# One maximum product with each score, and the pieces beside the attention at other steps

## The reference, cut to what matters

```
x = x + tanh(g_xattn) * xattn(layernorm(x), ctx, ctx)      # 16 heads of 16
x = x + tanh(g_ffn)   * ffn(layernorm(x))
# xattn: q, k, v = projections; softmax(q k^T / 4) v, per head
# ffn:   q, k by weights and rope; softmax(q k^T / 4) v; Wo; rmsnorm;
#        shared SwiGLU + the two best of 8 experts; rmsnorm
```

## Time and profile before

| what | value |
|---|---|
| median of 3 runs | 774.14 us (774.02 to 775.43) |
| the profiled execution | 774.76 us |
| its span, first to last instruction | 772.7 us |
| PE busy | 738.2 us (96%) |
| DVE, ACT, POOL busy | 515.0, 408.4, 218.6 us |
| matmul instructions | 3490 |
| score and maximum products | 512 each |
| granted TensorE clock, mean over the span | 0.991 |

### The profile page before, as it was taken

How to read it: one execution, slowest core, us unless ns; L and a number is a source line. 1 busy time by engine, 2 the same in 40 slices (tenths; PEclk the granted TensorE clock), 3 DMA queues, 4 the chain that set the end, 5 groups by cost and what they waited for, 6 DMA issues and landing times.

```text
span 772.7 us, 10296 instructions
## 1 busy us (share of the span) xinstructions
PE 738.2 (96%) x3490; PEld 334.7 (43%) x3490; DVE 515.0 (67%) x774; ACT 408.4 (53%) x768; POOL 218.6 (28%) x327
## 2 busy tenths in 40 slices
PE   8869999999999999999999999999999999999995
PEld 5522343243233233233423332333544756468884
DVE  5769848956978878887797789771566222533765
ACT  4447868777767776875775867666211122222000
POOL 5332233214305414313321420010104631400444
PEclk9979999999999999999999999999999999999998
DMA  8782234316214513512331232005102565000011
GB/s 262 226 228 80 60 107 127 83 32 202 69 42 150 151 42 112 159 45 78 110 99 44 97 110 68 17 2 166 53 0 97 186 192 179 9 1 0 30 40 42
DMA packets 51891, 73.31 MB, mean 95 GB/s; under 512 B 7808, under 2 KB 42880, under 8 KB 51840
## 3 DMA queue, kind: packets, MB, share of 16 engines
q1 hardware_dynamic: 47248, 63.80, 28.3%
q0 software_dynamic: 2816, 8.46, 2.9%
q10 hardware_dynamic: 1776, 0.40, 0.3%
HBM read 45.04 MB, written 27.33 MB: 94 GB/s over the span
## 4 chain that ended last, share of the span: by engine, by line
PE 75%; DVE 13%; ACT 5%; issue 3%; DMA 2%; POOL 0%; SPq 0%; POOLq 0%; DVEq 0%; ACTq 0%
PE ps L1514 35%; PE ps L1667 12%; PE ps L1697 12%; PE ps L1639 10%; DVE negm L1161 7%; ACT hS L912 3%; PE ps L1509 2%; DVE bst L1039 2%; PE ps L1573 1%; PE ps L1653 1%; DMA w<-mTs 1%; DMA rows<-in_L_xattn_wq_dram 1%; PE ps L1568 1%; DMA w<-scrq 1%; DVE rows L1046 0%
## 5 line engine op out<-in xcount | busy, mean ns | idle before, releaser
L1161 DVE TENSOR_REDUCE negm<-ps 128x2 f32<-128x1024 f32 x256 | 303.6, 1221 | 72.3 <-PE ps L1639 64.9
L912 ACT ACTIVATE hS<-ps 128x512 f32<-128x512 f32 x512 | 280.7, 604 | 119.4 <-PE ps L1697 117.5
L1697 PE MATMUL ps<-w 98*128 98x512 bf16 x512 | 171.1, 386 | 10.7 <-DMA w<-mTs 5.8
L1639 PE MATMUL ps<-w 96*128 96x512 bf16 x512 | 154.5, 383 | 6.4 <-DVE negm L1161 4.5
L1667 PE MATMUL ps<-hS,mix 128*17 128x512 f32 x1024 | 134.7, 598 | 0.2
L1697 PEld LDWEIGHTS ps<-w 98*128 98x128 bf16 x512 | 44.0, 97 | 163.4 <-ACT hS L912 77.1
L1639 PEld LDWEIGHTS ps<-w 96*128 96x128 bf16 x512 | 47.6, 99 | 59.6 <-DVE negm L1161 11.9
L1361 DVE SCALAR_TENSOR_TENSOR ctxs<-qk,ps 128x512 f32<-128x512 f32 x32 | 22.0, 688 | 71.1 <-ACT qk L948 46.7
L948 ACT ACTIVATE qk<-ps 128x512 f32<-128x512 f32 x32 | 19.1, 597 | 75.8 <-PE ps L1514 72.4
L1514 PE MATMUL ps<-w,hS 128*128 x256 | 55.6, 379 | 0.0
L1514 PEld LDWEIGHTS ps<-w,hS 128*128 128x128 f32 x256 | 48.6, 190 | 7.0 <-issue 0.5
(11 more groups left out here) (215 smaller groups left out, 848.1 us busy)
## 6 DMA issues: line engine op xcount, KB each, us to landing
w<-scrq SPq DMA_DIRECT2D x32, 384.0 KB, 4.2
scrk<-mix SPq DMA_DIRECT2D x24, 256.0 KB, 2.2
scrq<-mix SPq DMA_DIRECT2D x16, 384.0 KB, 3.4
scrq<-mix SPq DMA_DIRECT2D x24, 256.0 KB, 2.5
w<-scrk SPq DMA_DIRECT2D x32, 192.0 KB, 2.9
w<-scrk SPq DMA_DIRECT2D x32, 128.0 KB, 3.0
w<-in_L_ffn_W_experts_dram SPq DMA_DIRECT2D x8, 512.0 KB, 8.1
mix<-scrf SPq DMA_DIRECT2D x4, 528.0 KB, 3.9
```

The costliest lines, as they stand in the source:

```text
L912: nc.scalar.activation(prob[:, kt % PROB_SLOTS, s % HG, :], slot_bank(("unit", u)), ACT.Exp, scale=SC).then_inc(s_exp, 1)
L1161: V.tensor_reduce(negm[:, gi % 2, h, 2 * t2:2 * t2 + 2], ps[:, bank:bank + 2, :], AX.X, ALU.max, negate=True).then_inc(s_re, 1)
L1639: last = MM(ps[:, bank + t, :], qs[0:STK, g, h, tt * P:(tt + 1) * P], ks[0:STK, g, h, :], start=True, stop=True)
L1697: MM(take(("unit", u)), ks[:, g, h, kt * P:(kt + 1) * P], qs[:, g, h, :], start=True, stop=True).then_inc(s_sT, 1)
```

## The change

Each of the two products of a pair goes behind its own score, where both stood behind the second one. The place in the ring is now taken for the first of them, one step earlier; DVE is told, as before, when the second is done. Three constants come one step earlier and one comes one step later. Some pieces of the three lists move; the rest stay.

```diff
-AT_COPY, AT_HEADS, AT_MAX, AT_ROWS = 4, 8, 9, 11
+AT_COPY, AT_HEADS, AT_MAX, AT_ROWS = 3, 7, 8, 12
...
+            half_of = {}
+            def max_half(q, t):
+                gi, p = divmod(q, PAIRS // NG)
+                g = gi % NG
+                h, tt = p // 2, 2 * (p % 2) + t
+                if t == 0:
+                    if p == 0:
+                        pe.wait_ge(s_stk[g], (gi // NG + 1) * 64)
+                    half_of[q] = ring_bank()
+                last = MM(ps[:, half_of[q] + t, :], qs[0:STK, g, h, tt * P:(tt + 1) * P], ks[0:STK, g, h, :],
+                          start=True, stop=True)
+                if t:
+                    last.then_inc(s_rf, 1)
...
                         q = u // 2 + LEAD
-                        if s % 2 and q < N_PAIRS:
-                            max_pair(q)
-                        if h == HG - 1 and (kt or gi):
+                        if q < N_PAIRS:
+                            max_half(q, s % 2)
+                        if h == 3 and (kt or gi):
```

More of the change, by code:

```diff
@@ L87, in hook @@
         HOOKS.setdefault((a // UNITS, a // STEPS % NG, a % STEPS), []).append(what)
[L89 to L100, removed]
@@ L101, in flamingo_block @@
-    FA_STEPS = [("fatile", 0, 12), ("faempty", 0, 12), ("faempty", 1, 15), ("fatile", 1, 15), ("faempty", 2, 19), ("fatile", 2, 19),
-        ("fatile", 3, 23), ("faempty", 3, 23), ("fastats", 0, 32), ("nf", 0, 43)]
+    CROSS_STEPS = [("stats", 0, -34), ("norm", 1, -20), ("norm", 0, -16), ("tile", 2, -12), ("empty", 2, -12), ("tile", 0, -11), ("empty", 0, -11), ("tile", 3, -7), ("empty", 3, -7), ("tile", 1, -6), ("empty", 1, -6), ("tile", 4, -5), ("empty", 4, -5), ("tile", 5, -5), ("empty", 5, -5), ("tile", 6, -4), ("empty", 6, -4), ("part0", 0, -3), ("part1", 0, 1), ("rest", 0, 1), ("empty", 8, 2), ("tile", 8, 2), ("part2", 0, 2), ("tile", 7, 3), ("empty", 7, 3), ("part0", 1, 3), ("rest", 1, 4), ("tile", 9, 5), ("empty", 9, 5), ("part1", 1, 8), ("part2", 1, 10)]
@@ new lines, in flamingo_block @@
+    SELF_STEPS = [("stats", 0, -28), ("norm", 1, -24), ("norm", 0, -23), ("empty", 0, -21), ("tile", 0, -21), ("tile", 1, -9), ("empty", 1, -8), ("tile", 4, -4), ("empty", 2, -3), ("empty", 4, -3), ("tile", 2, -3), ("empty", 3, -2), ("tile", 3, -2), ("tile", 5, -1), ("empty", 5, 0), ("sum", 0, 1), ("tile", 6, 2), ("empty", 6, 2), ("sum", 1, 2), ("tile", 7, 2), ("empty", 7, 2), ("rest", 0, 2), ("rest", 1, 3), ("part0", 0, 5), ("tile", 8, 6), ("empty", 8, 6), ("part0", 1, 7), ("part2", 1, 10), ("part1", 1, 15), ("part2", 0, 16), ("part1", 0, 18)]
@@ L104, in flamingo_block @@
+    FA_STEPS = [("fatile", 0, 10), ("faempty", 0, 10), ("faempty", 1, 12), ("fatile", 1, 12), ("faempty", 2, 13), ("fatile", 2, 13), ("fatile", 3, 19), ("faempty", 3, 19), ("fastats", 0, 29), ("nf", 0, 44)]
     SELF_NO = {m: sum(k_ == "s" for k_, _ in INST[:m + 1]) for m in range(NI)}
@@ L1628, in ring_bank, with max_pair @@
                 return bank
-            def max_pair(q):
+            half_of = {}
+            def max_half(q, t):
                 gi, p = divmod(q, PAIRS // NG)
                 g = gi % NG
[L1633 to L1641, removed]
+                h, tt = p // 2, 2 * (p % 2) + t
[7 more added lines that the diff above has]
+                    last.then_inc(s_rf, 1)
+            def max_pair(q):
+                max_half(q, 0)
+                max_half(q, 1)
             def turn_max(gi):
```

## The result

The changed kernel takes 791.81 us (median of four runs, 791.25 to 794.65) against 774.32 us for the kernel before on the same chip: a ratio of 1.023, 95% interval 1.0214 to 1.0246, 17.5 us slower. The forecast had the sign and half the size (782.3, range 768 to 789).

What follows compares the result with a forecast made beforehand. The prediction took latency where PE, DVE and ACT meet as the bound. Its terms, 2 - 1.6 + 3.7 + 2.2 + 2.4 + 0.5 = +9.2 us, gave 784.0, 783.3 as median, less 1 us: 782.3, range 768 to 789.

Steps and rivals of the forecast that it cites:

- Part 1, the split: Product pairs split between two scores in 30 groups: 2 us gained, 4.2 us lost to later ring order, sum +2.
- The ring's cost: First product asks for its place before the odd score: 0.21 us lost in 20 of 30 groups, 4.2 us.
- Part 1, the heads: Heads turned before score 8 instead of between scores 8 and 9: no cost of their own counted.
- Part 2: Cross-instance preparation: sums copied at step 3 (-1.0) and tile 8 at step 6, tile 3 moved (-0.6); sum -1.6 us.
- Part 3, tile 7: Tile 7 at step 2 holds up ACT and delays the turn: +0.9 us in each of four instances, +3.7.
- Part 4, norms: Norms at steps 40 and 41, tile 0 at 43 waiting 0.55 us for the last norm: +2.2 us over four instances.
- Part 5, the rows' DMA: Issued at step 12, it meets SP's loads in the fourth and fifth instance, losing 1.2 us each: +2.4.
- Part 6, output tiles: Self-attention steps 10, 12, 13: tile 2 0.4 us too early for ACT's copy, step 19's wait goes; three times, +0.5.
- 1 us off, since engines catch up: Taken off the whole sum, as each term counts its wait as lost in full: 783.3 to 782.3 us.
- the faster one: Rival: even score spacing relieves ACT and DVE, 767 us; decided by a tile 8 stall under 0.2 us; chance 0.27.
- The DMA late everywhere: Rival: rows' DMA lands 3.0 us behind issue, 0.6 us lost in some 24 groups, 796 us; chance 0.06.
- That nothing comes of it: Rival: gains meet half the losses and no DMAs collide, within 0.2% of 774 us; chance 0.11.

Runs made afterwards that it cites:

- split_heads8: The kernel before with only the pair of products split, heads still at step 8 behind the score and ahead of the half product: 776.62 us, ratio 1.0030.
- halves_consts: The kernel before with the split and all four changed constants (3, 7, 8, 12), lists as before: 789.82 us, ratio 1.0200.
- after_three_back: The changed kernel with the rows' DMA back at step 11, and norms, tile 0 and output tiles at their old steps: 781.04 us, ratio 1.0103.
- halves: The kernel before with the split and the heads turned at step 7, other constants and all lists as before: 780.83 us, ratio 1.0089.
- rows12: The kernel before with only the rows' DMA moved to step 12: 777.62 us, ratio 1.0042.
- after_heads8: The changed kernel with the heads turned at step 8, behind the score and ahead of the half product: 786.37 us, ratio 1.0165.
- norms: The kernel before with only both norms and tile 0 moved to steps 40, 41 and 43: 783.49 us, ratio 1.0135.
- tiles_paired: The kernel before with tiles 5 and 7 at step 2, 6 and 8 at step 6, the rotated sum of k at step 7: 776.49 us, ratio 1.0047.

## Why the prediction was right in sign and short in size

The steps in order, by their own terms.

- **Part 1, the split: +2 forecast, 2.6 measured (split_heads8).** The ring's cost is what was worked out: by the starts of the scores, 18 stretches of four steps lose 0.2 us or somewhat more, 4.2 us in all. The gain of 2 us came too, but not from where it was looked for: changing kinds saves nothing (score and half product start 0.22 us apart, at 265.74, 265.96, 266.18 and 266.40 in the changed kernel), and 2.6 us come back at other steps, 0.2 at a time, such as steps 4 to 7 and 48 to 55 of the second instance (the rest is about 0.01 in each of many stretches). That this term fits is in part luck. The new wait of 0.3 us ahead of the turn came and costs nothing, as said.
- **Part 1, the heads: 0 forecast, and this was wrong.** The text turned the heads before score 8 and counted only that PE's order changed. What it cost once ACT ran dry wasn't asked: 9.0 us in the kernel before, 4.2 with the split, some 1.6 in the six instances of the whole change that the DMA doesn't touch.
- **Part 2: -1.6 forecast, about half of it seen.** From score 0 to 12 the two instances that prepare a cross instance are 0.46 us shorter each (15.24 to 14.78), as forecast 0.5, though the split alone takes off 0.22 of it. Tile 3's move, by the changed kernel against halves_consts, takes 0.5 us off four steps of the last group and adds it to the next four: 0.
- **Part 3, tile 7: +3.7 forecast, and the sign was wrong.** Each stall of ACT came at its place, but 1.06 us of tile was counted that runs beside tile 6. Steps 0 to 12 keep their length in two of the four instances; alone, the move gains 1.1 us (773.63 to 772.56), 2.3 with the copy behind exponential 3.
- **Part 4, norms: +2.2 forecast, some 1.8 measured** in the changed kernel. It holds only in this order; alone, the move costs 9.9.
- **Part 5, the rows' DMA: +2.4 forecast, 6.8 to 7.2 measured, and this is the term that took the forecast out of its range.** The place was right (fourth and fifth instance, and no other), and so were the 2.0 us for a quiet group (1.98 to 2.04 in most). Two things failed. The landing under SP's loads was taken as 3.5 us, which it was in the kernel before (3.29 and 3.50), but it was 3.93 and 4.64 in the changed one. And the stall was priced as itself, though behind the longer one the clock stayed at its lower level for 6.5 us, which cost 2.0 us more. Why the landing differs so much under like loads stays open. Where part 5 cites the Trainium skill, DMA: Bandwidth & Descriptors, section "Anatomy of one DMA", that section gives its 2.0 us for DMAs that GpSimd issues; this one is issued by ACT, and the trace has the same 2.0 us for it.
- **Part 6, output tiles: +0.5 forecast, some 1.8 measured.** Tile 2's wait was in the sum. That the earlier statistics make the ring late for step 34 was taken as 0: the half product there waits 0.95 us for DVE (at 402.78 in the sixth instance), steps 32 to 35 are 1.1 us longer in each of three instances, and in two of them 0.6 of it isn't given back.
- **1 us off, since engines catch up.** They don't: where terms meet they cost more or less than alone (16.0 and 13.3 give 17.5).

The runs that undo the change piece by piece give a sum that closes, each against the kernel before beside it. Parts 1 to 3, with the moves of the splitting pieces: 4.1 forecast, 7.1 measured (after_three_back). Parts 4 and 6: 2.7 forecast, 3.7 measured. Part 5: 2.4 forecast, 6.8 measured. That is 17.5 us, where the forecast had 9.2 less 1. So it was short by 4.4 us in the DMA, 3.0 in the first three parts, 1.0 in the norms and output tiles, and 1.0 in what was taken off. Without the first of these the time would have been within the range. Within the first three parts the overpriced tile 7 hid part of the loss: the heads and the new wait for ACT's copy of a tile stand on the other side (of that wait's 1.04 us, 0.4 are left in each of four instances beside halves). How much each is worth there stays open to about 1 us.

Of the rivals, the faster one was refuted by the stalls of ACT: tile 8 waits 0.37 us, over the 0.2 from which it was to be decided. The DMA late everywhere was not seen: it waits in two instances, and lands in 2.0 us elsewhere, short of the 2.3 where the loss would begin. That nothing comes of it was refuted by the 17.5 us. The first and last parts kept their length (0.7 us less ahead of the first score, 0.1 us more behind the last).

## What to carry to other kernels

When work is moved ahead of the next score, ask what the engine that lives on scores does meanwhile, even if the moving engine's own order costs nothing. A small transfer that is due is safer ahead of large ones than behind them: here it landed in 2.0 us without loads beside it and in up to 6.1 with them. A stall of 2 us on TensorE can cost as much again in the clock behind it (2.3 and 2.0 us here). Before adding the times of two products, look at which rows they contract over.

## What the runs showed of the hardware

- Two fp32 products of 64 rows each, over different halves of the partitions and neighbours in the program, run side by side: 1.06 us for both, 1.06 for one alone.
- A DMA of 8 KB issued by ACT lands 1.98 to 2.04 us behind its issue in groups without loads beside it. Beside SP's loads it took up to 6.10 us (3.29 and 3.50 in rows12, 3.93 and 4.64 in the changed kernel, 6.10 in halves_consts), and at times no longer than alone: in the fourth instance 3.93 us in the changed kernel and 2.04 in after_heads8, both issued at 261.76, with SP's loads issued within 0.1 us of the same times. Its landing can't be planned closer than that here.
- Behind PE's stall of 2.2 us the granted clock was 0.50 and 0.51 for 6.5 us. The length of the stall alone doesn't say whether that happens: in norms the clock was lower behind two stalls of 1.62 us and kept its level behind two of 1.55 and 1.54; in after_heads8 it was lower for 3.4 us behind one of 1.80, and in the changed kernel it was not behind 1.51 us at 265.74. Behind stalls of about 1 us (rows12) it was not lowered.
- Alternating between stationary operands of 98 and 96 rows at each product neither costs nor saves: 0.22 us from start to start, as for two alike.
- A CAST of DVE that takes 0.17 us by itself took 1.60 us and 2.12 us (tiles_paired) beside a POOL instruction, and both ended within 0.05 us of it.
